# A graph layer in groups of 1664 edges: query products spread among the scan transposes, the histogram ahead of the window sums, and a one-hot matrix built on ScalarE

## The reference

```
h = relu(layernorm(x))
Q, K, V = h @ Wq + bq, h @ Wk + bk, h @ Wv + bv        # 8 heads of 16
scores = sum(Q[dst] * K[src], -1) / 4 + (edge_attr @ We + be)
probs = softmax of scores over the edges of one dst     # with segment_max
x = x + segment_sum(probs * V[src], dst) @ Wo + bo
h = relu(layernorm(x))
hw = logmap0(h) @ W.T + b
deg = in-degree + out-degree (at least 1), dinv = deg ** -0.5
x = x + expmap0(segment_sum(hw[src] * dinv[src] * dinv[dst], dst))
```

## Time and profile before

| | before |
|---|---|
| time, median of 3 runs | 1495.47 us (1495.43 to 1497.34) |
| the profiled execution | 1495.77 us, of which the span of the records is 1493.8 us |
| first layer's loop | from about 60 us to about 971 us of the span |
| one step of the loop, L1011 to L1011 | 28.1 us |
| PE, DVE, ACT, POOL busy | 946.3, 740.5, 391.2, 595.5 us |
| TensorE's granted clock, mean | 0.678 of 2.4 GHz |

### The profile page before, as it was taken

One profiled execution on the slowest core, in us unless ns is written; L12 is line 12 of the kernel. 1 busy time (PEld: TensorE's weight loads), 2 busy tenths in 40 slices (PEclk: granted clock), 3 DMA queues, 4 the chain that ended last, 5 costly groups with the idle time before them and its releaser, 6 DMA issues.

```text
span 1493.8 us, 22198 instructions
## 1 busy us (share of the span) xinstructions
PE 946.3 (63%) x5820; PEld 805.1 (54%) x5820; DVE 740.5 (50%) x2771; ACT 391.2 (26%) x1107; POOL 595.5 (40%) x629
## 2 busy tenths in 40 slices
PE   5355775775775775675675676733757756765775
PEld 2244664664664564564564565622656645654665
DVE  8344544544554554553553553583534544454454
ACT  1502212212212212211311311142323423432341
POOL 0544454354354354354354354005343443444341
PEclk9655566566566566566566566675867877877787
DMA  5622232232232232233232233012011111111111
GB/s 150 178 80 83 87 104 82 84 104 83 81 106 86 77 110 86 72 111 89 71 112 89 70 110 93 6 47 87 26 41 34 40 40 37 37 40 40 33 41 29
DMA packets 87848, 111.23 MB, mean 74 GB/s; under 512 B 20787, under 2 KB 65791, under 8 KB 87807
## 3 DMA queue, kind: packets, MB, share of 16 engines
q0 software_dynamic: 26624, 68.20, 15.8%
q1 hardware_dynamic: 61191, 42.64, 9.9%
HBM read 99.83 MB, written 10.95 MB: 74 GB/s over the span
## 4 chain that ended last, share of the span: by engine, by line
PE 33%; DVE 24%; issue 20%; another core or an unknown queue 19%; DVEq 2%; DMA 1%; SPq 0%; ACT 0%
PE ps_q L1547 10%; PE ps_q L1673 3%; PE ps_q L1698 3%; PE ps_s L1673 3%; PE ps_c L1531 3%; DVE sc L933 2%; DVE wv L1275 2%; PE ps_f L1601 2%; PE ps_f L1600 1%; DVE fwd_reset L1274 1%; DVE prod L927 1%; PE ps_c L1527 1%; DVE oh_lo L897 1%; PE ps_b L1673 1%
## 5 line engine op out<-in xcount | busy, mean ns | idle before, releaser
L662 POOL DMA_INDIRECT kv<-kv_tab,idx x416 | 396.6, 953 | 533.8 <-DVE wv L1004 367.6
L695 POOL DMA_INDIRECT kv<-hs_tab,idx x208 | 198.6, 955 | 335.9 <-PE ps_q L1682 191.6
L1369 ACT ACTIVATE S<-iota,nloc 128x128 f32<-128x128 f32 x384 | 122.0, 389 | 636.1 <-remote 635.0
L1547 PE MATMUL ps_q<-qwin,ST 128*128 128x128 f32 x832 | 207.0, 432 | 19.5 <-DVE prod L927 10.5
L1547 PEld LDWEIGHTS ps_q<-qwin,ST 128*128 128x128 f32 x832 | 187.1, 331 | 20.8 <-DVE prod L927 10.8
L1580 PE MATMUL ps_f<-oh_lo,oh_hi 128*50 128x64 bf16 x416 | 83.4, 301 | 96.2 <-issue 96.0
L927 DVE TENSOR_TENSOR prod<-kv,ps_q 128x512 f32<-128x512 f32 (+1 forms) x128 | 74.6, 583 | 140.2 <-issue 58.8
L1011 DVE TENSOR_SCALAR fb<-ps_c 128x8 f32<-128x8 f32 x32 | 5.3, 166 | 274.3 <-remote 267.3
L1559 PE MATMUL ps_r<-wv,S 128*128 128x137 f32 x832 | 140.1, 341 | 1.8 <-DVE wv L1004 1.8
L1559 PEld LDWEIGHTS ps_r<-wv,S 128*128 128x128 f32 x832 | 140.0, 253 | 2.1 <-DVE wv L1004 2.1
L1580 PEld LDWEIGHTS ps_f<-oh_lo,oh_hi 128*50 128x50 bf16 x416 | 54.2, 172 | 110.4 <-issue 109.4
(11 more groups left out here) (257 smaller groups left out, 1715.6 us busy)
## 6 DMA issues: line engine op xcount, KB each, us to landing
dloc_b<-dloc_tab SPq DMA_DIRECT2D x32, 416.0 KB
kv<-kv_tab,idx POOLq DMA_INDIRECT x416
attr_s<-in_attr SPq DMA_DIRECT2D x32, 192.0 KB
kv<-hs_tab,idx POOLq DMA_INDIRECT x208
kv_tab<-qkv SPq DMA_DIRECT2D x5, 640.0 KB, 4.0
x_tab<-x SPq DMA_DIRECT2D x32, 64.5 KB, 1.7
qwin<-q_tab SPq DMA_DIRECT2D x32, 64.0 KB
xwin<-in_x SPq DMA_DIRECT2D x32, 64.0 KB
```

Source lines behind the costliest of these rows:

```text
L662: pool.indirect_dma_start(out=kv[:, b, t, :], out_offset=None, in_=kv_tab, in_offset=bass.IndirectOffsetOnAxis(ap=idx[:, b, t:t + 1], axis ...
L695: pool.indirect_dma_start(out=kv[:, j, t, 0:D], out_offset=None, in_=hs_tab, in_offset=bass.IndirectOffsetOnAxis(ap=idx[:, j, t:t + 1], ax ...
L1369: A.activation(S[:, b, t, :], iota[:], ACT.Abs, bias=nloc[:, g, t:t + 1] if known(g) else nloc[:, bass.ds(g, 1), t:t + 1].rearrange("p g t ...
L1547: mm = M.matmul(ps_q[c % 2][:, (t - t0) * D:(t - t0 + 1) * D], ST[:, b, t, :], qwin[:, b, :], start=True, stop=True)
```

## The change

It touches the loop of the first layer only.

- The query products get four PSUM tiles (`ps_q[0..3]`, which take the place of two `ps_q` and two `ps_s`), one for each chunk. Chunk c of group g waits for product c of group g-1 instead of product c-2 of its own group. `p_bias` moves to the last of them, so L1565 no longer waits for the sum of the scores (`s_sc`).
- In PE's step g, chunk 0 of group g+1 stands between the first two scan transposes, chunk 1 between the next two (behind L1590), chunk 2 behind the output matmuls, then all of the bias, then chunk 3. Nothing of `query(g)` is left at the start of step g.
- The histogram becomes the first work of a step, ahead of the window sums, and writes into a part of `ps_r`. DVE's `add_counts(g)` comes before `backward(g)` instead of before `factor(g)`.
- `row_one_hots` moves from DVE to ACT: one pass Abs and one pass Relu over 128 x 1664, with a wait between them, at the start of ACT's step, two groups ahead. ACT's third part of `one_hots` moves behind the exponential.
- SP loads `dloc_b` one group further ahead, at the start of its turn.

The diff, cut to SP's wait, `row_one_hots` (gone from DVE's program, new in ACT's), ACT's step, the wait in PE's `query`, and PE's step:

```diff
-                wait_apart(sp, s_st, g - 1, (s_base, 1))
+                wait_apart(sp, s_sta, g - 1, (s_base, 1))
...
-            def row_one_hots(g, b):
-                dve.wait_ge(s_dlocb[b], 16 * ((g - b) // 2 + 1) if known(g) else (g + (2 - b)) * 8)
-                if not (known(g) and g < 2):
-                    dve.wait_ge(s_qt, NCH * (g - 1))
-                V.tensor_scalar(ST[:, b].rearrange("p t e -> p (t e)"), dloc_b[:, b, :], imj[:, 0:1], None, ALU.is_equal)\
-                    .then_inc(s_st, 1)
+            def row_one_hots(g, b):
+                act.wait_ge(s_dlocb[b], 16 * ((g - b) // 2 + 1) if known(g) else (g + (2 - b)) * 8)
+                if not (known(g) and g < 2):
+                    act.wait_ge(s_qt, NCH * (g - 1))
+                rows = ST[:, b].rearrange("p t e -> p (t e)")
+                A.activation(rows, dloc_b[:, b, :], ACT.Abs, bias=nrow[:]).then_inc(s_sta, 1)
+                act.wait_ge(s_sta, g + 1)
+                A.activation(rows, rows, ACT.Relu, bias=1.0, scale=-1.0).then_inc(s_st, 1)
...
             def step(g, b, nodes=True, more=True, far=True):
+                if far:
+                    row_one_hots(g + 2, b)
                 if more:
-                    one_hots(g + 1, 1 - b, (0, 1))
+                    one_hots(g + 1, 1 - b, (0,))
                 if nodes:
                     agg_copy(g - 1)
                 if more:
-                    one_hots(g + 1, 1 - b, (2,))
+                    one_hots(g + 1, 1 - b, (1,))
                 carry_factor(g)
                 weights(g)
+                if more:
+                    one_hots(g + 1, 1 - b, (2,))
...
-                    if not (known(g) and g == 0 and c < 2):
-                        pe.wait_ge(s_prod, NCH * g + c - 1)
+                    if not (known(g) and g == 0):
+                        pe.wait_ge(s_prod, NCH * (g - 1) + c + 1)
...
             def step(g, b, edges=True, nodes=True, more=True):
                 if edges:
-                    query(g, b, (2, 3))
+                    histogram(g, b)
                 if nodes:
-                    window_sums(g - 1, 1 - b, edges)
+                    window_sums(g - 1, 1 - b)
                 if edges:
                     pe.wait_ge(s_v1, g + 1)
                     M.transpose(p_v1, f1[:, :, T - 1], ident[:]).then_inc(s_v1T, 1)
+                    if more:
+                        query(g + 1, 1 - b, (0,))
                     wait_apart(pe, s_cf, g + 1, (s_part, 1))
                     M.transpose(p_c1, c1[:, b, 0:P], ident[0:H, 0:H]).then_inc(s_cfT, 1)
                 if nodes:
                     pe.wait_ge(s_agn, g)
                     M.transpose(ps_f[:, 0:D], agn[:], ident[:]).then_inc(s_agTp, 1)
                 if edges:
+                    if more:
+                        query(g + 1, 1 - b, (1,))
                     pe.wait_ge(s_v2, g + 1)
...
                 if edges and more:
-                    query(g + 1, 1 - b, (0,))
-                    bias(g + 1, 1 - b, (0, 1))
-                    query(g + 1, 1 - b, (1,))
-                    bias(g + 1, 1 - b, (2, 3))
+                    query(g + 1, 1 - b, (2,))
+                    bias(g + 1, 1 - b, (0, 1, 2, 3))
+                    query(g + 1, 1 - b, (3,))
```

More of the change, by code:

```diff
@@ L304, in build @@
         e_od = sb("e_od", [P, 2])
[L306 to L307 removed]
+        ps_q = [pb(f"ps_q{i}", [P, 512]) for i in range(NCH)]
+        ps_s = ps_q[2:]
         ps_b = pb("ps_b", [P, 512])
@@ L555, in _, with turn @@
                 sp.dma_start(x2_tab[N:NPAD, :], zero_rows[:]).then_inc(s_pad, 16)
[L556 to L560, removed]
+                def turn(g, b, more=True):
+                    if more:
+                        load_dloc(g + 1, 1 - b)
+                    load_edges(g, b)
+                    store_nodes(g - 2, b)
+                    load_nodes(g, b)
+                with sp.Fori(1, GROUPS // 2 - 1) as n:
+                    turn(2 * n, 0)
+                    turn(2 * n + 1, 1)
+                turn(GROUPS - 2, 0)
+                turn(GROUPS - 1, 1, more=False)
                 store_nodes(GROUPS - 2, 0)
@@ L1064, in step @@
                     edge_one_hots(g + 1, 1 - b, s_S, TA)
-                    row_one_hots(g + 1, 1 - b)
                 if edges:
+                    add_counts(g)
                     backward(g, b, A)
@@ L1409, in _ @@
             with act.If_eq(in_order, 1):
+                row_one_hots(0, 0)
+                row_one_hots(1, 1)
                 step(0, 0, nodes=False)
-                with act.Fori(0, GROUPS // 2 - 1) as n:
+                step(1, 1)
+                with act.Fori(1, GROUPS // 2 - 1) as n:
+                    step(2 * n, 0)
                     step(2 * n + 1, 1)
-                    step(2 * n + 2, 0)
-                step(GROUPS - 1, 1, more=False)
+                step(GROUPS - 2, 0, far=False)
+                step(GROUPS - 1, 1, more=False, far=False)
                 agg_copy(GROUPS - 1)
@@ L1541, in query, with histogram, window_sums @@
                     t0, t1 = CH[c]
[L1542 removed]
+                    if c == 0:
                         pe.wait_ge(s_st, g + 1)
[L1544 to L1545 removed]
+                    if not (known(g) and g == 0):
+                        pe.wait_ge(s_prod, NCH * (g - 1) + c + 1)
                     for t in range(t0, t1):
[L1547 removed]
+                        mm = M.matmul(ps_q[c][:, (t - t0) * D:(t - t0 + 1) * D], ST[:, b, t, :], qwin[:, b, :],
                                       start=True, stop=True)
                     mm.then_inc(s_qt, 1)
[L1551 removed]
+            def histogram(g, b):
+                pe.wait_ge(s_oh, 2 * g + 2)
+                if not (known(g) and g == 0):
+                    pe.wait_ge(s_od, g)
+                for t in range(T):
+                    mm = M.matmul(p_od, oh_hi[:, b, :, t], oh_lo[:, b, :, t], start=(t == 0), stop=(t == T - 1))
+                mm.then_inc(s_hist, 1)
+            def window_sums(g, b):
                 pe.wait_ge(s_wv, 2 * g + 1)
```

37 lines of the change are left out of this document (14 added, 23 removed).

## The result

| | before | after |
|---|---|---|
| median of 6 runs of each | 1495.45 us (1494.24 to 1497.34) | 1488.54 us (1486.91 to 1491.03) |
| span of the profiled execution | 1493.8 us | 1486.4 us |
| ratio | 1 | 0.9956, 95% interval 0.9943 to 0.9969 |

The change makes the kernel 0.44% faster; the forecast was 1493 us. The time is 1.9 us more than the span before and 1.8 us more after, so the spans show the whole difference. The experiments ran on other chips of the same kind, and two sorts turned up among them: on two chips the kernel before takes 1495.6 and 1507.8 us, and on two others 1044 us. I call them **held** and **free** chips; each experiment says on which it ran. The pair above comes from a held one.

A forecast was written before the change was run, and what follows sets the result against it. A step was bounded by a fixed 18.5 us from burst to release plus a 9.55 us serial chain. Terms of -0.05 us times 29 (-1.5), -2 and +0.5 took 1495.8 to 1493 us; 8-in-10 range 1456 to 1512, forecast alone 1488 to 1499.

The forecast's parts named there:

- Burst start to release is fixed: First layer's loop: from a burst's first gather to the end of DVE's `s_rc` wait, 18.5 us, whenever PE ends.
- ST off DVE, -0.95: DVE after the release: without the row one-hot comparison, the sum R comes earlier, -0.95 us a step up to the backward scan.
- Chunk 1 eats it, +0.08 net: PE behind L1590: chunk 1's four matmuls take 1.7 us and delay the scan, using up the 0.95 us; +0.08 us net.
- add_counts, -0.13: End of DVE's chain: moved ahead of `backward`, its 0.13 us are hidden by chunk 1; -0.13 us a step.
- Chunk 0 and ACT at nothing: PE's chunk 0 between transposes and ACT's two one-hot passes are covered by the burst's wait; cost 0.
- rival B: PE in the chain: chunks 0 and 1 keep its clock at 2.4 GHz, 1.3 us a step gained, 1456 us; chance 0.08.
- Rival C: PE's transposes come later: chunk 0 not out at release, scan 0.55 us behind; +0.45 us a step, 1506 us; chance 0.14.
- Rival D: ACT late: the burst holds chunk 3's signal, `row_one_hots` starts only at the release; +0.8 us a step, 1516 us; chance 0.12.
- "Gain 0" for PE's earlier end: Histogram and chunks 0, 1 leave the step's start; window sums start 1.7 us earlier, but the release stays: gain 0.
- PE's end 9.0 us into the burst: PE's last matmul before the release (L1567 before the change) was put at 9.0 us behind the burst's first gather.
- The last step with edges, -2: Last step with edges, no burst or queries: the scan's 1.9 us wait for the transpose behind the histogram goes; -2 us.
- Rival A: First layer's loop: PE's end does set the release, so its earlier end gives 1.1 us a step, 1461 us; chance 0.14.

The follow-up runs named there:

- the split burst: Changed kernel with the last 5 of 13 first-layer gathers waiting for `s_rc`: 1302.94 us, ratio 0.8635 (held chip); 946.44 us, 0.9063 (free chip).
- the third kernel: Changed kernel with the row one-hots back on DVE as one comparison: 963.88 us, ratio 0.9242 to the kernel before, on a free chip.
- the second kernel: Kernel before with only the row one-hots moved to ACT, with SP's earlier load: 1044.35 us, ratio 1.0004, on a free chip.

## Why the prediction was right

**Right, by its own steps**, all on held chips:

- *Burst start to release is fixed*: 18.55 us before and after, 18.8 with PE 2 us later. And it is the burst: 11.7 us with 8 gathers in a row, whether PE ends at 5 us or at 10.
- *ST off DVE, -0.95*: the sum R starts 0.75 us behind the release (452.02 - 451.27), against 1.75: -1.00.
- *Chunk 1 eats it, +0.08 net*: L985 at 4.79 us, against 4.74: +0.05. Taking chunk 1 out gave 0.93 us of the step back. That this came so near is partly luck, as two errors cancel: the chunk starts 0.27 us behind the start of L1611 and not at its end, so L1616 starts 4.21 us behind the release in place of 4.4 to 4.5; and the scan follows L1616 by 0.58 us, not by less than 0.55 as I had it for a transpose behind other matmuls.
- *add_counts, -0.13*: weighing starts 7.49 us behind the release, against 7.60 (462.81 below, less 455.21 of the earlier trace rows): -0.11 in all, so -0.16 behind the scan.

```profile
462.81 1.94 DVE L1004 TENSOR_TENSOR wv<-kv,wv 128x1024 f32<-128x1024 f32 x2
```

- *Chunk 0 and ACT at nothing*: chunk 0 is out before the release; ACT's passes (1.68 and 1.59 us, 1.55 estimated) lie 5 to 8.4 us into the burst and it idles 10 us behind them. By the Trainium skill ("ScalarE: Activation LUTs", Rules for kernel authors) a pass is estimated at 1.7 us; the trace agrees.
- *Clock (rival B)*: 0.50, the lower level, in the chain, before and after. *Rival C*: chunk 0 is cut up late in the burst, but out at the release; its other half, the scan 0.55 us behind the transpose, did come (0.58). *Rival D*: no ACT pass behind the release, though the passes start 5.1 us into the burst, where D was to decide. The 10 us of idle time behind them show that this line was drawn far too early.

A like step gains 0.09 us in place of 0.05: -2.5 us for 28 of them, -1.5 predicted.

**Mis-sized, or missed.** By its own bounds for a step, the forecast's lower end is 1495.8 - 5.2 - 2 + 0.5 = 1489.1 us and not 1488; the measured 1488.5 lies at that edge.

- *"Gain 0" for PE's earlier end* failed in one step of 29. I had read the release as held to the burst's end wherever in it PE ends, because that was so from 8.95 us on the earlier trace rows; with L1595 at 6.45 us the signal got through at 9.95. This step alone gave 3.2 us, more than all that was forecast, and is most of the difference between 1493 and 1488.5; without it the total would lie at 1492. The three traces of the changed kernel on held chips have it alike: PE at 4.8, 6.5 and 7.2 us, release after 8.6, 9.95 and 14.3, and the step takes 24.5 to 24.7 us, against 27.6 and 27.7 in the two traces of the kernel before. Why it gets through there is open. PE's end alone isn't the reason, since with the split burst a matmul at 4.6 us still waited to 11.5.
- *PE's end 9.0 us into the burst* was put too early. The window sums start 1.4 us earlier than before (4.15 us in the mean, against 5.59; 1.7 predicted), but take 5.24 us in place of 4.38, as more of them runs at the lower clock: the granted clock is 0.53 in the sums at 464.91 after and 0.63 in those at 470.40 before. So the matmul comes at 8.8 to 10.3 us, all of it held. Nothing in the sum hung on it.
- *The last step with edges, -2*: that term came out at -0.8 (13.0 us from its release to the next in place of 13.8, as the transpose is no longer behind the histogram). The total behind the last burst is near the forecast (-1.5) by other terms: the last release that a burst holds is followed by the next after 18.9 us in place of 20.3 (no burst there, so PE's shorter way counts: -1.4, not in the sum), and at the very end DVE waits 2.42 us for the output matmuls in place of 1.68 (+0.7).
- *The first step, +0.5*: +0.4 from its burst to the next (33.3 us in place of 32.95).
- *SP's earlier load costs 0*: it does, but it isn't the 3 us ahead that I gave it. It ends ACT's wait in 21 steps (5.9 us at most), in place of chunk 3's signal. ACT's idle time covers it.
- *"What holds them I don't know"*: nor does it show itself now, but its bounds do (below).

So the reasoning holds for the 28 like steps, and the total came out faster than forecast mostly by terms that weren't in the sum.

**Rival A** (PE's end counts) was given 0.14 and 1461 us. It is wrong in size on held chips, where a part of it arrived in that one step, and right on free ones, where the same edit gives 100 us. The page that it names (the Trainium skill, "SBUF — State Buffer", Who interferes with whom: a DMA doesn't contend with a compute engine) speaks of the ports of the on-chip memory. Nothing in the traces of the free chips is against it. On the held ones signals and starts come late beside gathers, but no run shows contention at a port, so "the trace contradicts the page" said more than the rows do. No row of the kernel before could tell which chip the next run meets; that such a thing can differ was not among my rivals.

## What to carry to other kernels

When a wait ends at a fixed distance from something that isn't its producer, change that something first: one more wait on the gather queue gave 13.2% on a held chip (1302.94 against 1500.81 us), and the whole change 0.5% there. The kernel with the split burst beats the kernel before on both sorts (0.8635 and 0.9063); on a free chip it is no faster than the changed kernel by the estimate above (946 and 947 us). And an edit that puts work under a stall isn't worthless, only hidden: chunks between transposes and a histogram ahead of the sums give 7.6% where nothing stalls (the third kernel), so measure such an edit on more than one chip before you drop or keep it.

## What the runs showed of the hardware

- **Two sorts of chip.** The same kernel takes 1495 to 1508 us on some and 1044 us on others. POOL's gathers take the same on both (0.95 us, one each 1.25 us). The gathers' transfers, too: the software queue's share is 18.0% of 1305.2 = 235 us on the held chip and 24.8% of 945.6 = 235 us on the free one, for the same kernel:

```profile
q0 software_dynamic: 26624, 68.20, 18.0%
```

```profile
q0 software_dynamic: 26624, 68.20, 24.8%
```

- **The hold.** On held chips PE, DVE or ACT first idles over 0.3 us ahead of an instruction with "issue" as the cause mostly 10 to 13.5 us into a burst of the first layer, and 5.7 to 7.8 us into one of the second; in the seven traces of free chips it shows in no burst. Signals are late sooner: by 3.1 to 3.4 us for a matmul that ends 5.2 to 6.8 us into the burst. The second layer's rows are half as long (512 of 1024 bytes) and its small matmuls are many. That speaks against the bytes as the cause; no experiment tests it. With 13 gathers the hold ends 2.5 us behind the last one, about the time that a gather takes to land on a free chip (2.5 us above); with 8 it ends 1.7 to 2.1 us behind. In it PE starts an instruction every 0.7 us or slower, as with the last of chunk 0 after (472.05, 472.76, 474.16, 474.86).
- **The held chips' traces have fewer semaphore events**: 8.5 to 8.9 thousand in all seven, 19.6 to 19.9 thousand in all seven of the free chips, of nearly the same programs. Most of the missing ones are those of transfers (4.8 thousand in the pair's trace before, 15.0 thousand in the second kernel's). So part of the "remote" there may be an event that wasn't recorded. A path for events that is full would fit the late signals too, but that is a guess. Nor can recording be left out as the cause of the hold: every execution timed here has a recorded span and clock, so there is no time without it.
- **The mean clock goes with it.** The kernel before has a mean granted clock of 0.67 to 0.68 on the held chips and 0.76 on the free ones.
